# Two-best experts of the last layer: tokens sorted into blocks by expert for 24 of 32 tiles

## The reference

```
def _L3_ffn_ref(x, gate_w, expert_w):
    xf = x.reshape(Bb * Tt, C)
    logits = xf @ gate_w.T
    w, sel = jax.lax.top_k(logits, TOP_K)
    w = jax.nn.softmax(w.astype(jnp.float32), axis=1)
    w_full = jnp.zeros((n, NUM_EXPERTS))
    w_full = w_full.at[jnp.arange(n)[:, None], sel].add(w)
    expert_out = jnp.einsum('nc,edc->ned', xf, expert_w)
    out = jnp.einsum('ne,ned->nd', w_full, expert_out)
...
x = x + _L3_ffn_ref(_layernorm(x, axis=-1), L3_ffn_gate_w, L3_ffn_expert_w)
```

## Time and profile before

| what | us |
|---|---|
| median of 3 runs | 3157.15 (3153.61 to 3160.93) |
| the profiled execution, its own time | 3158.02 |
| span of its trace | 3156.2 |
| of this, from the last stage's first instruction to the end | 243.5 |
| mean granted TensorE clock of the execution, as a share of full speed | 0.979 |

### The profile page before, as it was taken

The page is one execution under the profiler, slowest core; times in us unless marked ns, Lnnn a source line. Parts: engine busy times, 40 slices in busy tenths (PEclk is TensorE's granted clock), DMA queues, the critical chain, the costliest instruction groups (busy, mean ns, idle before and its releaser), DMA issues. The chain is left out here.

```text
span 3156.2 us, 65764 instructions
## 1 busy us (share of the span) xinstructions
PE 3005.2 (95%) x27034; PEld 2224.1 (70%) x27034; DVE 2173.1 (69%) x6079; ACT 1122.1 (36%) x1963; POOL 892.8 (28%) x921
## 2 busy tenths in 40 slices
PE   8998999999899989888999999999999979998999
PEld 6776766666577755667888888888888866776444
DVE  5666356111376789566999989999999983666666
ACT  5654211222466679443222222222222204554000
POOL 1322000233222222002444544444444441332000
PEclk9999999999999999999999999999999979999999
DMA  4010120243410000411000000000000011010000
GB/s 138 29 42 30 57 69 21 74 121 92 120 42 29 16 12 1 147 46 59 5 4 6 5 5 5 5 6 5 5 4 6 5 31 55 29 42 2 14 20 21
DMA packets 79242, 112.36 MB, mean 36 GB/s; under 512 B 11872, under 2 KB 62304, under 8 KB 78560
## 3 DMA queue, kind: packets, MB, share of 16 engines
q1 hardware_dynamic: 71760, 98.58, 9.4%
q0 software_dynamic: 6144, 8.52, 1.4%
q10 hardware_dynamic: 1040, 1.05, 0.1%
HBM read 87.03 MB, written 21.10 MB: 34 GB/s over the span
## 5 line engine op out<-in xcount | busy, mean ns | idle before, releaser
L2193 POOL TENSOR_TENSOR pk_hisig<-pk_hihot,pk_sigs 128x512 f16<-128x512 f16 x512 | 520.8, 1044 | 664.2 <-DVE pk_hihot L2469 663.0
L2291 PE MATMUL pk_ps<-X,dw_downT 128*128 128x256 f32 x2048 | 480.3, 385 | 0.0
L2337 PE MATMUL pk_ps<-ew_up,pk_act_h 128*128 128x256 f32 x2048 | 461.2, 384 | 1.7 <-DVE pk_act_h L2457 1.7
L2337 PEld LDWEIGHTS pk_ps<-ew_up,pk_act_h 128*128 128x128 f32 x2048 | 390.3, 192 | 57.6 <-issue 2.0
L2291 PEld LDWEIGHTS pk_ps<-X,dw_downT 128*128 128x128 f32 x2048 | 380.9, 191 | 60.0 <-issue 14.8
L667 DVE TENSOR_REDUCE a_mx<-a_ps_s 128x8 f32<-128x1024 f32 x192 | 226.3, 1221 | 206.9 <-PE a_ps_s L503 183.2
L2201 ACT ACTIVATE pk_act_h<-pk_ps 128x512 f32<-128x512 f32 x256 | 152.9, 598 | 546.2 <-PE pk_ps L2291 546.2
L2470 DVE TENSOR_TENSOR pk_lohot<-pk_iota_h,pk_ps 128x1024 f16<-128x1024 f16 x256 | 310.4, 1213 | 0.0
L340 ACT ACTIVATE a_pT<-a_ps_s 128x512 f32<-128x512 f32 x384 | 198.0, 605 | 91.4 <-PE a_ps_s L520 91.3
L2671 PE MATMUL mo_ps<-mw_we,mo_xnT 128*128 128x512 f32 x512 | 224.6, 596 | 0.0
L2457 DVE TENSOR_TENSOR pk_act_h<-pk_act_h,pk_ps 128x512 f32<-128x512 f32 x256 | 171.5, 680 | 61.2 <-PE pk_ps L2321 61.2
(11 more groups left out here) (380 smaller groups left out, 5216.2 us busy)
## 6 DMA issues: line engine op xcount, KB each, us to landing
ro_w<-in_L_W SPq DMA_DIRECT2D x16, 1024.0 KB, 7.3
i_ctx_t<-in_ctxT SPq DMA_DIRECT2D x16, 512.0 KB, 3.9
i_side<-in_side SPq DMA_DIRECT2D x16, 512.0 KB, 4.8
row_dram<-sh_row SPq DMA_DIRECT2D x8, 512.0 KB, 3.0
sum_dram<-sh_new SPq DMA_DIRECT2D x8, 512.0 KB, 2.9
X<-sum_dram SPq DMA_DIRECT2D x4, 1024.0 KB, 9.3
wa_ctx_t<-in_ctxT SPq DMA_DIRECT2D x8, 512.0 KB, 4.1
dw_downT<-in_L_downT SPq DMA_DIRECT2D x1, 4096.0 KB, 14.8
```

Of the source, the lines that this page charges most:

```text
L2193: ins = pool.tensor_tensor(hisig[:, buf, n, :, :, :], hi, sig2.broadcast_to([P, TP, 2, ECH]), ALU.mult)
L2291: ins = pe.matmul(hid.bank(f"h{c}")[:, j * 2 * P:(j + 1) * 2 * P], downT[:, k, e * P:(e + 1) * P], XT[:, p, k, :], start=(k == 0), stop=(k ...
L2337: ins = pe.matmul(tail.bank("y")[:, 0:D], act_h[:, p % 2, c, s * P:(s + 1) * P], up[:, c, :], start=(c == 0), stop=(c == ECH - 1))
```

## The change

Groups 0 to 5 (24 tiles) no longer go through all experts. They form three chunks of two groups. For each chunk DVE computes for every token and each of its two experts a row number in a table of 24 blocks of 128 rows, in which each block belongs to one expert (`ranks`, `blocks`; the counts over the tokens of a tile come from two small products on PE). POOL scatters the normalized rows to these places in a DRAM table `sent` (48 indirect transfers in all). SP loads the table back two blocks (a *pair*) at a time, PE transposes them, reads the number of each block's expert into a register, and multiplies each block by that expert alone. ACT copies both the transposes and the results from PSUM, SP stores the results in a second table `made`, and POOL gathers each token's two results (48 transfers), which DVE adds to `X` with their weights (`sums`). A chunk always runs 12 pairs, whatever the tokens chose. Groups 6 and 7 stay dense: 6 ahead of the first chunk, 7 behind the last. The tables `sent` are set to zero in the stage `product_key_experts`, by three transfers that SP issues ahead of three of the loads of `xo`. The products of the dense groups now go round two PSUM banks instead of four.

```diff
+MOE_SENT = 6
+MOE_SIDE = 2
+MOE_CHUNKS = MOE_SENT // MOE_SIDE
+MOE_PAIRS = (2 * MOE_SIDE * G + MOE) // 2
+MOE_BLOCKS = 2 * MOE_PAIRS
+MOE_REGION = MOE_BLOCKS * P
+MOE_AHEAD = 3
...
+        xt = Relay(f"{tag}_xt", sem, banks[0:2])
+        lt = Relay(f"{tag}_lt", sem, banks[2:3])
+        small = Relay(f"{tag}_small", sem, banks[3:4])
+        main = Relay(f"{tag}_main", sem, banks[4:6])
+        ys = Relay(f"{tag}_ys", sem, banks[6:8])
...
+        routed = (0, 1, 6, 2, 3, 4, 5, 7)
...
+            for g in range(MOE_SENT):
+                pool.wait_ge(pos_ready, g + 1)
+                for u in range(G):
+                    for n in range(2):
+                        pool.indirect_dma_start(
+                            out=sent[g // MOE_SIDE][:, :], in_=xn[:, g, u, :], in_offset=None,
...
+            for g in range(MOE_SENT):
+                c = g // MOE_SIDE
+                if g % MOE_SIDE == 0:
+                    for s in range(4):
+                        pool.wait_ge(kept[s], 16 * len([n for n in range((c + 1) * MOE_PAIRS) if n % 4 == s]))
+                if g >= 2:
+                    pool.wait_ge(sums_ready, g - 1)
...
+            def turned(c, p):
+                n = c * MOE_PAIRS + p
+                dst = xt.empty(pe)
+                pe.wait_ge(loaded[n % (MOE_AHEAD + 1)], 16 * (n // (MOE_AHEAD + 1) + 1))
+                for h in range(2):
+                    for k in range(KC):
+                        at = (h * KC + k) * P
+                        ins = pe.transpose(dst[:, at:at + P], xb[:, n % (MOE_AHEAD + 1), h, k * P:(k + 1) * P], ident[:, :])
+                turn_use[n] = xt.filled(ins)
+
+            def experts_of(c, p):
+                return [pe.value_load(table[0:1, c, j:j + 1], min_val=0, max_val=MOE - 1)
+                        for j in (2 * p, 2 * p + 1)]
+
+            def products(c, p, experts):
+                n = c * MOE_PAIRS + p
+                dst = ys.empty(pe)
+                xt.wait_taken(pe, turn_use[n])
+                for h in range(2):
+                    for k in range(KC):
+                        ins = pe.matmul(dst[:, h * D:(h + 1) * D], xbT[:, n % 2, h, k, :],
+                                        we[:, k, bass.ds(experts[h], 1), :].rearrange("p e n -> p (e n)"),
+                                        start=(k == 0), stop=(k == KC - 1))
+                ys.filled(ins)
...
+            for c in range(MOE_CHUNKS):
+                pe.wait_ge(table_ready, c + 1)
+                turned(c, 0)
+                experts = experts_of(c, 0)
+                for p in range(MOE_PAIRS):
+                    if c == 0 and p in (0, 4):
+                        columns(4 + p // 4)
...
+                    if p + 1 < MOE_PAIRS:
+                        turned(c, p + 1)
+                        ahead = experts_of(c, p + 1)
+                    products(c, p, experts)
+                    experts = ahead
+            for u in range(G):
+                all_experts(7, u)
...
+            def sums(g):
+                dve.wait_ge(gathered[g % 2], 2 * 16 * G * (g // 2 + 1))
+                for n in range(2):
+                    for u in range(G):
+                        t = g * G + u
+                        ins = dve.scalar_tensor_tensor(X[:, t, :], got[:, g % 2, u, n, :], pair[:, g, n, u:u + 1],
+                                                       X[:, t, :], ALU.mult, ALU.add)
...
+            for c in range(MOE_CHUNKS):
+                sp.wait_ge(sent_done[c], 16 * 2 * MOE_SIDE * G)
+                for p in range(MOE_AHEAD):
+                    load(c, p)
+                for p in range(MOE_PAIRS):
+                    if p + MOE_AHEAD < MOE_PAIRS:
+                        load(c, p + MOE_AHEAD)
+                    keep_rows(c, p)
...
+                if t >= 2 and t - 2 < len(blank):
+                    rows = blank[t - 2].rearrange("(p r) n -> p r n", p=P)
+                    sp.wait_ge(zero_ready, 1)
+                    sp.dma_start(rows, zero[:, :].rearrange("p (a n) -> p a n", a=1).broadcast_to(rows.shape)).then_inc(
+                        blanked, 16)
```

More of the change, by code:

```diff
@@ L2172, in _ @@
             late.load(sp)
+            sp.wait_ge(blanked, 16 * len(blank))
         @block.gpsimd
@@ L2544, with __init__, empty, filled @@
 MOE = 8
-def top2_experts(nc, keep, w, out):
+MOE_SENT = 6
[5 more added lines that the diff above has]
+MOE_AHEAD = 3
+class Relay:
+    def __init__(self, name, sem, banks):
+        self.banks = banks
+        self.full = sem(name + "_full")
+        self.taken = [sem(f"{name}_taken{b}") for b in range(len(banks))]
+        self.made, self.read = 0, 0
+    def empty(self, pe):
+        n, size = self.made, len(self.banks)
+        if n >= size:
+            pe.wait_ge(self.taken[n % size], n // size)
+        return self.banks[n % size]
+    def filled(self, ins):
+        ins.then_inc(self.full, 1)
+        self.made += 1
+        return self.made - 1
+    def arrived(self, eng):
+        eng.wait_ge(self.full, self.read + 1)
+        return self.banks[self.read % len(self.banks)]
+    def take(self, ins):
+        ins.then_inc(self.taken[self.read % len(self.banks)], 1)
+        self.read += 1
+        return self.read - 1
+    def wait_taken(self, eng, n):
+        eng.wait_ge(self.taken[n % len(self.banks)], n // len(self.banks) + 1)
+def top2_experts(nc, keep, w, out, sent):
     tag = "mo"
@@ new lines, in all_experts @@
+            def all_experts(g, u, between=None):
+                for q in range(MOE // 2):
+                    dst = main.empty(pe)
+                    for k in range(KC):
+                        ins = pe.matmul(dst[:, :], xnT[:, slot_of(g), k, u * P:(u + 1) * P],
+                                        we[:, k, 2 * q:2 * q + 2, :].rearrange("p e n -> p (e n)"),
+                                        start=(k == 0), stop=(k == KC - 1))
+                    main.filled(ins)
+                    if q == 1 and between is not None:
+                        ranks(between)
@@ L2676, in _ @@
             columns(0)
-            gate_logits(0, 0)
+            logits(0)
             turned_logits(0)
-            turns(pe, turn)
+            columns(1)
+            logits(1)
+            ranks(0)
+            turned_logits(1)
+            columns(6)
+            logits(6)
+            ranks(1)
+            turned_logits(6)
+            columns(2)
+            all_experts(6, 0)
+            logits(2)
+            turned_logits(2)
+            all_experts(6, 1, between=2)
+            columns(3)
@@ L2761, in _ @@
-            norm(0)
-            weights(0, 0)
-            turns(dve, turn)
+                step(dve.tensor_copy(top_f[:, :, :], top_i[:, :, 0:2]))
+                h = hot[:, g % 2 if g < MOE_SENT else 2, :, :, :]
+                for n in range(2):
+                    ins = dve.tensor_tensor(h[:, n, :, :], over_experts(top_f[:, :, n]), part[:, :, :], ALU.is_equal)
+                step(ins)
+                if g < MOE_SENT:
+                    dve.tensor_tensor(both[:, g % 2, :, :], h[:, 0, :, :], h[:, 1, :, :], ALU.add).then_inc(
+                        hot_ready, 1)
@@ new lines, in _ @@
+            layer_norm_scale(None, dve, keep, rstd, rstd_sq, setup)
+            norm(0)
+            norm(1)
+            dve.wait_ge(consts, 4)
+            weights(0)
+            norm(6)
+            ranks(0)
+            weights(1)
+            norm(2)
+            ranks(1)
+            blocks(0)
+            weights(6)
+            norm(3)
+            all_experts(6, 0)
+            weights(2)
+            ranks(2)
+            all_experts(6, 1)
+            norm(4)
+            weights(3)
@@ new lines, in _ @@
+            ranks(3)
+            blocks(1)
+            all_experts(6, 2)
+            norm(5)
+            all_experts(6, 3)
+            dve.sem_inc(out_ready, 1)
+            norm(7)
+            for g in (4, 5):
+                weights(g)
+                ranks(g)
+            blocks(2)
+            weights(7)
+            for g in range(4):
+                sums(g)
+            all_experts(7, 0)
+            all_experts(7, 1)
+            sums(4)
+            all_experts(7, 2)
+            all_experts(7, 3)
```

411 lines of the change are left out of this document (273 added, 138 removed).

## The result

The changed kernel takes 3161.71 us (median of 20 runs, 3154.52 to 3165.60) and the kernel before, run beside it, 3155.47 (20 runs, 3152.08 to 3160.93): ratio 1.0015, 95% interval 1.0008 to 1.0021. By the medians that is 6.2 us slower, just inside the 0.2% that the prediction calls no change; by the ratio's interval 2.5 to 6.6 us. The predicted 3168 us is 6 us too high, and the range (3134 to 3205) holds the result.

A forecast was written before the change was run, and what follows sets the result against it. PE alone bounds the stage before; PE's queue was to set the pace after. 2912.7 + 73.8 + 20 + 36 x 3.34 + 40.5 = 3167.2, plus 0.9: 3168 us, range 3134 to 3205.

The forecast's parts named there:

- The array, 2.47 us a pair: PE's array after the change: four transposes at 0.52 us and four products at 1.95 us, 88.9 us for 36 pairs.
- PE's queue, 3.34 us a pair: PE's instructions per pair: array 0.33, waits 0.15, eight register instructions 0.96, two reads 1.90 us; said to set the pace.
- first rival: PE's queue between transposes and products: reads are cheap, the array sets the pace at 2.47 us a pair, time 3137; chance 0.24.
- The loads, costed at nothing: Transfers of 256 KB for the pairs: 3.0 us to landing, three pairs ahead, said to fit under PE's queue.
- pairs paced by a load's landing: Sign named in advance: pairs whose pace is set by a load's landing would show the prediction wrong outright.
- Between and in the chunks: Around the pairs: two boundary waits 9.0 us, shared PSUM banks 7.5, the array's tail and start 3; together about 20 us.
- To the first pair: From the stage's start to the first pair's transposes: DVE's queued work and dense group 6, 73.8 us.
- after the last product: End of the stage: dense group 7, the stall for group 4's rows, last sums, store and handovers, 40.5 us.
- the zeroing transfers: Three transfers of 3.1 MB ahead of loads of `xo`: some 19 us each, covered; at most 57 us if not.
- POOL late at the end: Final gathers beside DVE's sums: issues taking twice as long put the end at 55 us, time 3182; chance 0.07.
- The clock falls: PE's clock during the pairs: if low, 4.94 us a pair and 3225; for half the pairs 3197; chance 0.08.

The follow-up runs named there:

- e9: The changed kernel with two pairs loaded ahead in three buffers, in place of three in four; 3198.69 us, ratio 1.0137 to the kernel before.
- e2: The changed kernel with each block's number read twice on PE, the second value unused; 3189.61 us, ratio 1.0109 to the kernel before.
- e4: The changed kernel with six pairs loaded ahead in place of three, and loads running on across chunk boundaries; 3132.48 us, ratio 0.9926 to the kernel before.
- e3: The changed kernel with six pairs loaded ahead in seven buffers, in place of three in four; 3139.87 us, ratio 0.9950 to the kernel before.
- e5: e4 without PE's reads of block numbers, experts being constants, so the output is not the reference's; 3124.44 us, ratio 0.9904 to the kernel before.
- e10: e6 with a chunk's first transposes ahead of the previous chunk's last products, and group 4's sums behind group 7's dense tiles; 3128.19 us.
- e12: e11 with two dense tiles of group 6 among chunk 0's pairs, and work for groups 4 and 5 four pairs later; 3132.02 us.
- e6: e4 with a pair's two reads ahead of its transposes in PE's queue, in place of behind them; 3128.06 us, ratio 0.9917 to the kernel before.
- e11: e10 with each read alone between groups of products, a pair ahead of its use; 3124.05 us, ratio 0.9900 to the kernel before.

## Why the prediction was right in the time and wrong in its reason

- **The array, 2.47 us a pair.** Too high: measured 2.17 start to start. The transposes add 0.44 to the products' 1.73, not 0.52 to 1.95: their records overlap, so that adding two busy times did not give the time from pair to pair.
- **PE's queue, 3.34 us a pair: the step that failed.** The term was mis-sized in the reads. The prediction took 0.95 for a read and four times 0.12 for its register instructions, 1.43 together, by POOL's issue as the nearest row; e9 gives 0.70 and up, with the changed kernel's own places 0.70 to 0.98. With its own 0.33 and 0.15 for the rest a pair's queue is then 1.9 to 2.4 us, about the array's pace and not 3.34. Four reads make it 3.3 to 4.4, where e2 measured 3.49. The Trainium skill (DMA: Bandwidth & Descriptors, section Latency and other measured facts) gives a floor of about 600 ns for such a load; the 0.70 to 0.98 with the register instructions lie above it and agree, and it would have been the better guide here than POOL's issue. The first rival's condition (two reads and eight register instructions under 2.56 us by its terms) thus held, though its time did not.
- **The loads, costed at nothing: the second step that failed, and it hid the first.** "Three pairs ahead" was a cover of 10 us only by the 3.34 us a pair that was wrong. At 2.2 to 2.4 three pairs are 6.5 to 7.3 us, and the rounds of chunk 2 take 10.4 to 11.5. A load lands in 3.1 us in the median while chunk 0 runs, as was assumed, but in 4.4 while chunk 2 does, beside POOL's gathers and the stores (2.8 to 5.3 in all); and it first has to wait for a store. So the first rival's 3137 did not come either. The prediction said that pairs paced by a load's landing would make it wrong outright: in chunk 2 they are.
- **Between and in the chunks, about 20 us.** The boundary waits are 4.56 and 3.93 us, where 4.5 was forecast, and e4 against e3 makes both together 9.2, where 9.0 was. What else lies between the pairs is 7.8 in e5 (85.9 less 36 times 2.17), where some 10.5 was. Right.
- **To the first pair 73.8, after the last product 40.5.** Measured 77.6 and 40.7. Right as sums; their terms were not measured one by one.
- **Costed at nothing, and so it is:** the zeroing transfers. The third layer's part around them keeps PE without a gap, and a transfer of 3 MB lands in 11.3 us, not 19:

```profile
1480.00:2550.00 1070.00, 1070.00 (x8172) 890.56 (x8171) 972.97 (x3481) 261.34 (x419) 489.75 (x482) 1.00 0.04 14
...
sent<-pk_zero SPq DMA_DIRECT2D x3, 3072.0 KB, 11.3
```

- **POOL late at the end.** Not in the changed kernel. Its last sixteen gathers stand 1.25 us apart, also where DVE adds, but for two that took 1.16 and 1.01 in place of the 0.95 of the earlier trace rows:

```profile
3129.89 3.38 DVE L3009 SCALAR_TENSOR_TENSOR X<-mo_got,mo_pair,X 128x256 f32<-128x256 f32 x8 [0.45 <-DMA mo_got<-made,mo_pos_i]
3130.83 1.16 POOL L2704 DMA_INDIRECT mo_got<-made,mo_pos_i  x1 [0.31 <-issue]
3132.29 1.01 POOL L2704 DMA_INDIRECT mo_got<-made,mo_pos_i  x1 [0.30 <-issue]
3133.60 0.95 POOL L2704 DMA_INDIRECT mo_got<-made,mo_pos_i  x1 [0.30 <-issue]
```

By the Trainium skill (SBUF — State Buffer, section Who interferes with whom) a DVE instruction with two inputs in SBUF, as these sums are, contends with a POOL instruction that reads SBUF, where the gathers' row numbers lie; these rows show 0.3 us of it at most, and no block. Once the pairs are faster (e5, e10, e12), gathers do hold the end, not because POOL is slowed but because DVE's queue puts `sums(3)` ahead of the dense tiles.
- **The clock falls.** In part. It does not stay low: products at the lower level follow the waits for loads at the boundaries and in chunk 2, and two pairs later they are back at 1.9 to 2.0 us. On the products its price is 7.4 us against e4 and 11.4 against e6.

Together: the pairs and what lies between them were put at 140.2 us and took 131.4. Of this 120.2 stood for a queue that sets the pace of every pair; at the array's 2.17 the pairs alone are 78.1, 42 us less. What was not in the sum, 16.7 us of reads that stand open in part and 19.6 of late loads with their clock, is 36. The time came out right by luck: two errors of opposite sign nearly met, and the mechanism that ran is not the forecast's.

## What to carry to other kernels

A look-ahead counted in items covers a latency only at the pace of the items: when a term makes them faster, or is found smaller than thought, work out the whole round again (issue, landing, compute, copy, and the store ahead of the next load in the same queue) and divide it by the items in flight. An idle time that a trace puts down to an engine's own issue may belong to a transfer that came just in time, so the open waits are a lower bound of what more look-ahead gains: here 12.0 us stood open, and e4, which ended them, gained 29. Ask at once which queue the saved time then runs into; here it was DVE's order at the end.

## What the runs showed that was not expected

A read of a number from SBUF into a PE register with its register instructions took 0.70 to 0.98 us when nothing hid it, and two more of them a pair cost 0.8 us a pair in e2 ((160.8 − 131.4) / 36). Two reads a pair that follow no late load still cost 0.46 us a pair (e4 against e5, 16.7 / 36). Whether PE's queue does not run far enough ahead of the array or single reads are too long for their cover is not shown; moving them (e6, e11) mostly moved the open time. Some took much longer, as this pair of e2 with 3.77 us ahead of its products, and no row says why; that is left open:

```profile
3132.75 0.60 PE L2829 MATMUL mo_ps<-ident,mo_xb 128*128 128x128 f32 x4
3137.12 3.78 PE L2842 MATMUL mo_ps<-mw_we,mo_xbT 128*128 x8 [3.77 <-issue]
```
